# A deformable-attention bias network on one core: every first-layer tile built as a sum and a relu, five of eight by GpSimd and three by VectorE

## The chip, the cores and the metric

The kernel runs on one core of a Trainium2 chip. The metric is the device time of one execution in microseconds. The core has five engines that work side by side and wait for one another on semaphores: TensorE (PE in the profile, its weight loads PEld), VectorE (DVE), ScalarE (ACT), GpSimd (POOL) and SyncE (SP), which here issues the transfers. Operands lie in SBUF (128 partitions); TensorE writes to PSUM (8 banks of 512 fp32 values per partition).

## The reference

The input x is 2 x 256 x 32 x 32. A first layer computes queries, then offsets for an 8 x 8 grid of sampling points per image and group (16 image-group pairs, "groups" below), samples the input there, and makes keys and values. The part that matters here is the position bias: for each of 16 groups, each of 1024 pixels i and each of 64 points j,

```
pos  = grid_q[i] - grid_kv[j]                      # two coordinates
bias = sign(pos) * log1p(|pos|)                    # two coordinates
bias = relu(bias @ cpb_w1 + cpb_b1)                # 2 -> 64 channels
bias = relu(bias @ cpb_w2 + cpb_b2)                # 64 -> 64
bias = bias @ cpb_w3 + cpb_b3                      # 64 -> 1
sim  = q k^T + bias ; softmax over j ; times v
```

Then come an output projection, an MLP with GELU, and a second layer with full self-attention over 1024 tokens, 8 heads of 32, two images. All data is fp32.

## The kernel before, in words

**Stages.** Lines are those of the profile. A head (queries, convolution of the offsets, sampling) fills the first 91 us. The bias network (the loop at L917 on TensorE, L481 on ScalarE, L678 on VectorE, L359 on GpSimd) follows, then the first attention (L935 on), projection and MLP (L986 on), and the second attention.

**First layer of the bias network.** x and y take 32 values per point along their axis, so channel c of pixel (row a, column b) and point j is u(j, b) + v(j, a), with u = w1x * s_x and v = w1y * s_y + b1, where s is the signed logarithm. A tile m (0 to 511, 32 per group) is 128 partitions x 1024 values: two points in the upper and lower 64 partitions, two more along the free axis, and half of the pixel rows (512 pixels). U and V2 (in SBUF, two buffers each for a piece of 16 tiles) hold u and v; ScalarE writes them in `first_sums` (L444). V1 (in PSUM) holds -v, written by ScalarE in `first_bounds` (L454).

**Two kinds of tile.** relu(u + v) = max(u, -v) + v. Even tiles use this: VectorE makes max(u, -v) in one operation (`bound1`, L668: u from SBUF, -v from PSUM), and TensorE adds the missing W2^T v to the second layer's sum with `offset` (L889), four bf16 matmuls with 57 rows, whose operands are the three-part bf16 split of the logarithms (S, 128 x 4096 bf16, filled by GpSimd at L342 and by six transfers at L263) and a matrix wl1 made in the head (L822, L593 to L599, L856, L654). The split itself is L646, L648, L649 and L651 on VectorE. In odd tiles GpSimd writes u + v to SBUF (L370, both inputs in SBUF), and VectorE applies the relu in place, SBUF to SBUF (`relu1`, L674).

**The rest of the loop.** `layer2` (L898) is four fp32 matmuls 64 x 64 x 512 per tile into z2, a ring of 3 x 2 banks; ScalarE's `relu2` (L479) reads it and writes h2, a ring of 8; for four tiles at a time `layer3` (L907) makes 16 fp32 matmuls into bank 7, and after 32 tiles VectorE copies that bank to BT (L692). h1, the ring between first and second layer, has 4 tiles (HRING). 

**What orders the work.** Each engine's program is written out in order of m. VectorE waits in `relu1(m)` for GpSimd's add (z1_added). GpSimd's add of tile m waits for `layer2` of tile m-4 (z2_ready, the ring) and, at L366, for VectorE's h1_ready of m-1, that is until the relu of tile m-2 is done:

```
                if m >= HRING:
                    pool.wait_ge(z2_ready, m - HRING + 1)
                if m >= 2:
                    pool.wait_ge(h1_ready, m - 1)
```

**In the head.** The sampling weights wsm (8 tiles k of 128 x 1024) are hat functions made by ScalarE (L436, L438), then multiplied by hx: k = 0 to 3 by GpSimd (L355), k = 4 to 7 by VectorE (L659), the latter behind the split of the logarithms in VectorE's program. TensorE takes each with 32 small matmuls (L868); after the last one kv_ready is set, on which keys and values (L466 to L474) and the loop depend. SP sends the logarithms to memory (L266) and reads them back broadcast (L256, raw), sends and places the bf16 parts (L260, L263), and then issues the late weights (L286).

Of the kernel before, what the change touches and what calls it, by code (L numbers as in the profile page):

```python
# [44 lines left out]
WS_POOL = 4  # L45
# [12 lines left out]
def build(nc, d, out):  # L58
# [5 lines left out]
    with ctx:  # L64
# [96 lines left out]
        def v(name, i=0, n=1):  # L161
# [4 lines left out]
        ld_vec, ld_bd, ld_w1, ld_late, ld_w2 = (sem(x) for x in ("ld_vec", "ld_bd", "ld_w1", "ld_late", "ld_w2"))  # L166
# [6 lines left out]
        grid_out, grid_in, w1p_ready, wl1_ready, wl1_saved = (sem(x) for x in ("grid_out", "grid_in", "w1p_ready", "wl1_ready", "wl1_saved"))  # L173
        pn_ready, ln_ready, sparts_ready, s_in = (sem(x) for x in ("pn_ready", "ln_ready", "sparts_ready", "s_in"))
        s_out = [sem(f"s_out{a}") for a in range(3)]
        ws_ready, kv_ready, kv_saved, k_ready, v_ready, k_saved, v_saved = (
            sem(x) for x in ("ws_ready", "kv_ready", "kv_saved", "k_ready", "v_ready", "k_saved", "v_saved"))
        abs_ready, hat_ready, ws_pool = sem("abs_ready"), sem("hat_ready"), sem("ws_pool")
        q_copied, qk_ready = sem("q_copied"), sem("qk_ready")
        raw_in, u_ready, v_ready1, z1_added, h1_ready, z2_ready, h2_ready, l3_done = (  # L180
            sem(x) for x in ("raw_in", "u_ready", "v_ready1", "z1_added", "h1_ready", "z2_ready", "h2_ready", "l3_done"))
        sf_ready, sf_out, fold_ready, fold_saved, neg_ready = (
            sem(x) for x in ("sf_ready", "sf_out", "fold_ready", "fold_saved", "neg_ready"))
# [39 lines left out]

        block = ctx.enter_context(nc.Block())
# [108 lines left out]
        def _(pool):  # L333
# [6 lines left out]
            pool.wait_ge(ld_vec, 64)  # L340
            for i in range(2):
                pool.tensor_copy(S[:, 8 * i:8 * (i + 1), :, :].rearrange("p g a b -> p (g a) b"),  # L342
                                 v("one_rows").unsqueeze(2).to_broadcast((P, 8 * CHUNKS, W))).then_inc(cleared, 1)


# [6 lines left out]

            for k in range(WS_POOL):
                pool.wait_ge(hat_ready, k + 2)
                pool.tensor_tensor(wsm[:, k, :], wsm[:, k, :], hx[:, :], ALU.mult).then_inc(ws_pool, 1)  # L355


            pool.wait_ge(kv_ready, 1)
            for m in range(1, PAIRS * G, 2):  # L359
                c, w, hf = m % PAIRS // 4, m % 4 // 2, m % 2  # L360
                if m % PIECE == 1:
                    pool.wait_ge(u_ready, 2 * (m // PIECE + 1))
                if m >= HRING:
# [3 lines left out]
                shape, i = (P, 2, HALF // W, W), m // PIECE % 2  # L367
# [807 lines left out]
```

## Time and profile before

| | |
|---|---|
| median of 3 runs | 1402.49 us (1401.1 to 1406.26) |
| the profiled execution | 1401.21 us, its span 1399.0 us |
| PE busy | 1302.2 us (93% of the span) |
| DVE, ACT, POOL busy | 921.5, 967.6, 748.9 us (66, 69, 54%) |
| mean granted TensorE clock | 0.974 |
| bias loop, from its first matmul (L889) to the last copy (L692) | 90.89 to 841.20 us |

The span runs from the first to the last instruction of the profiled execution; 2.2 us of its time lie around it. PE's busy share is that of the modelled matmul ends. PEclk is the granted TensorE clock in tenths of full speed. "Idle before" names the time in which an engine stood still just before an instruction, and behind the arrow what released it.

### The profile page before, as it was taken

The page shows a single profiled execution, that of the slowest core. Times are in us where ns is not written, and L with a number is a line of the kernel's source. Part 1 is how long each engine was busy: PE and PEld are TensorE (multiplying, and loading weights), DVE is VectorE, ACT ScalarE, POOL GpSimd, SP SyncE. Part 2 cuts the span into 40 slices and gives each one's busy share as a digit, 9 for nine tenths or more (in the row PEclk, how much of TensorE's full clock was granted, in tenths as well). Part 3 has the DMA queues.
Part 4 walks back from the last instruction along what each step waited for, and adds up shares of the span by engine and source line. Part 5 has one row for each costly group of instructions (what it writes and reads, how often), then busy time and mean ns, then how long its engine had stood idle before and what let it go on. Part 6 is the DMA issues. An engine that isn't in the chain of part 4 may idle for free.

```text
span 1399.0 us, 29958 instructions
## 1 busy us (share of the span) xinstructions
PE 1302.2 (93%) x11666; PEld 616.0 (44%) x11666; DVE 921.5 (66%) x1270; ACT 967.6 (69%) x1263; POOL 748.9 (54%) x681
## 2 busy tenths in 40 slices
PE   3169999999999999999999998799997999999998
PEld 2132222222222222222222226444454888888885
DVE  6876666666666666666666657410037999999995
ACT  3377777777777777777777773332204999999994
POOL 4166666666666666666666652200000767777772
PEclk9579999999999999999999999999999999999999
DMA  2141110111011101110111000000007222212211
GB/s 69 54 134 31 31 32 2 31 31 32 2 31 32 29 4 32 31 26 7 31 32 23 9 1 1 1 0 0 0 29 272 62 60 60 54 45 52 60 30 60
DMA packets 19922, 53.27 MB, mean 38 GB/s; under 512 B 4642, under 2 KB 7330, under 8 KB 19668
## 3 DMA queue, kind: packets, MB, share of 16 engines
q1 hardware_dynamic: 19824, 51.92, 14.1%
q8 instruction: 70, 1.15, 0.4%
q14 instruction: 24, 0.20, 0.0%
q10 hardware_dynamic: 4, 0.01, 0.0%
HBM read 40.95 MB, written 10.95 MB: 37 GB/s over the span
## 4 chain that ended last, share of the span: by engine, by line
PE 80%; DVE 11%; issue 3%; ACT 2%; POOL 2%; DMA 1%; SPq 1%; DVEq 0%; ACTq 0%; POOLq 0%
PE ps L898 31%; PE ps L907 17%; PE ps L889 5%; DVE aneg L773 5%; PE ps L1055 4%; PE ps L1063 4%; PE ps L1004 4%; PE ps L1014 4%; PE ps L1047 3%; DVE conv L620 2%; PE ps L1038 1%; DVE big L776 1%; POOL big L355 1%; PE ps L1026 1%; PE ps L991 1%
## 5 line engine op out<-in xcount | busy, mean ns | idle before, releaser
L898 PE MATMUL ps<-big,w 64*64 64x512 f32 x4096 | 483.5, 589 | 0.0
L479 ACT ACTIVATE big<-ps 128x1024 f32<-128x1024 f32 x256 | 262.0, 1023 | 179.0 <-PE ps L898 179.0
L674 DVE TENSOR_SCALAR big<-big 128x1024 f32<-128x1024 f32 x256 | 177.8, 694 | 263.8 <-POOL big L370 263.8
L668 DVE TENSOR_TENSOR big<-qpad,ps 128x1024 f32<-128x1024 f32 x256 | 311.0, 1215 | 7.8 <-ACT ps L458 5.4
L370 POOL TENSOR_TENSOR big<-qpad 128x1024 f32<-128x1024 f32 x128 | 244.5, 1910 | 133.2 <-PE ps L898 68.6
L370 POOL TENSOR_TENSOR big<-qpad,V 128x1024 f32<-128x1024 f32 x128 | 244.5, 1910 | 129.7 <-PE ps L898 73.5
L479 ACT ACTIVATE big<-ps,vec 128x1024 f32<-128x1024 f32 x256 | 284.0, 1109 | 0.0
L390 POOL TENSOR_TENSOR big<-BT,big 128x512 f16<-128x512 f32 x129 | 150.4, 1166 | 248.0 <-DVE big L776 248.0
L907 PE MATMUL ps<-big,w3s 128*32 128x512 f32 x2048 | 246.2, 598 | 1.3 <-ACT big L479 1.3
L898 PEld LDWEIGHTS ps<-big,w 64*64 64x64 f32 x4096 | 146.6, 133 | 205.9 <-issue 112.6
L773 DVE TENSOR_REDUCE aneg<-ps 128x1 f32<-128x1024 f32 x131 | 158.3, 1209 | 6.0 <-PE ps L1047 5.7
L535 ACT ACTIVATE big<-ps,aneg 128x1024 f32<-128x1024 f32 x130 | 148.5, 1142 | 6.0 <-DVE aneg L773 5.3
L1055 PE MATMUL ps<-ident,big 128*128 128x128 f32 x1032 | 136.3, 274 | 3.8 <-DVE big L779 3.8
L907 PEld LDWEIGHTS ps<-big,w3s 128*32 128x32 f32 x2048 | 53.5, 109 | 181.7 <-ACT big L479 92.2
L1055 PEld LDWEIGHTS ps<-ident,big 128*128 128x128 f32 x1032 | 121.1, 141 | 23.2 <-DVE big L779 5.7
L1063 PE MATMUL ps<-BT,big 128*128 x2048 | 115.6, 208 | 1.1
L1063 PEld LDWEIGHTS ps<-BT,big 128*128 128x128 f16 x2048 | 99.0, 97 | 21.3 <-issue 10.3
L889 PE MATMUL ps<-S,wl 57*64 57x512 bf16 x1024 | 102.3, 389 | 1.5 <-ACT vs L474 1.5
L1047 PE MATMUL ps<-h1l,h1h 128*128 128x512 f32 x262 | 94.5, 443 | 6.8 <-DMA h1l<-k_d 5.2
L889 PEld LDWEIGHTS ps<-S,wl 57*64 57x64 bf16 x1024 | 29.5, 105 | 144.7 <-ACT big L479 80.7
L779 DVE SCALAR_TENSOR_TENSOR big<-ps,big 128x512 f16<-128x512 f32 x129 | 89.1, 691 | 0.8 <-ACT big L543 0.4
L540 ACT ACTIVATE BT<-ps 128x512 f32<-128x512 f32 x129 | 79.1, 613 | 4.0 <-PE ps L1055 4.0
(140 smaller groups left out, 1116.5 us busy)
## 6 DMA issues: line engine op xcount, KB each, us to landing
raw<-s_f SPq DMA_DIRECT2D x32, 512.0 KB, 6.1
h1h<-q_d SPq DMA_DIRECT2D x64, 128.0 KB, 3.0
h1l<-k_d SPq DMA_DIRECT2D x64, 128.0 KB, 3.1
q_d<-XN SPq DMA_DIRECT2D x8, 512.0 KB, 2.6
k_d<-XN SPq DMA_DIRECT2D x8, 512.0 KB, 2.6
X<-in_x SPq DMA_DIRECT2D x2, 1024.0 KB, 6.3
out<-X SPq DMA_DIRECT2D x8, 256.0 KB, 2.0
m<-grid_d SPq DMA_DIRECT2D x1, 1024.0 KB, 4.6
```

Of the source, the lines that this page charges most:

```text
L370: pool.tensor_tensor(h1[m % HRING].rearrange("p (y a b) -> p y a b", y=2, b=W), u.unsqueeze(2).to_broadcast(shape), a[:, :, HALF // W * hf ...
L390: pool.tensor_tensor(PTL[u % 2][:, 0:HALF], PF[u % 2], PTH[u % 2][:, 0:HALF], ALU.subtract).then_inc(pFl_ready, 1)
L479: act.activation(h2[m % H2RING], z2[m % ZRING], ACT.Relu, bias=v("cb2") if m % 2 else 0.0).then_inc(h2_ready, 1)
L535: act.activation(PR[u % 2], bank(2 * (u % 2), 2), ACT.Exp, bias=aneg[u % 2][:, :]).then_inc(pr_ready, 1)
L668: dve.tensor_tensor(h1[m % HRING].rearrange("p (y a b) -> p y a b", y=2, b=W), u.unsqueeze(2).to_broadcast(shape), b[:, :, HALF // W * hf: ...
L674: dve.tensor_scalar(h1[m % HRING], h1[m % HRING], 0.0, None, ALU.max).then_inc(h1_ready, 1)
L773: dve.tensor_reduce(aneg[u % 2][:, :], bank(2 * (u % 2), 2), AX.X, ALU.max, negate=True).then_inc(mx_ready, 1)
L889: pe.matmul(z2[m % ZRING][CH * y:CH * (y + 1), HALF * x:HALF * (x + 1)], wl1[CH * x:CH * x + KROWS, 2 * w + y, :], S[CH * x:CH * x + KROWS ...
L898: last = pe.matmul(z2[m % ZRING][CH * y:CH * (y + 1), HALF * x:HALF * (x + 1)], w2[CH * x:CH * (x + 1), :], h1[m % HRING][CH * x:CH * (x + ...
L907: last = pe.matmul(zb[32 * k:32 * (k + 1), :], w3s[:, a:a + 32], h2[(m + k // 2) % H2RING][:, HALF * (k % 2):HALF * (k % 2 + 1)], start=(m ...
L1055: last = pe.transpose(bank(4 + hf)[:, P * i:P * (i + 1)], PR[u % 2][:, P * jt:P * (jt + 1)], ident[:, :])
L1063: last = pe.matmul(bank(6 + u % 2)[:, 0:VW], pT[u % 2][:, P * jt:P * (jt + 1)], V3[:, 2 * k + u // NK, jt, :], start=(jt == order[0] and p ...
```

## The change

It drops the max trick and its bf16 product. Every tile is now u + v followed by `relu1` on VectorE. Of each eight tiles, numbers 1, 4 and 6 have their sum made by VectorE (`add1`: u from SBUF, +v from V1 in PSUM), the other five by GpSimd (both inputs in SBUF). VectorE issues the sum of tile m+1 ahead of the relu of tile m. The ring h1 grows from 4 to 6 tiles (a new buffer h1x). GpSimd no longer waits for VectorE's relu; it waits for the ring and for its own previous sum. `relu2` has the bias in every tile. In the head the fold of w1y through W2, the matrix wl1, the three-part split, its six placing transfers and S are gone, and all eight products of wsm go to VectorE.

```diff
-HRING, H2RING, BURST, ZRING = 4, 8, 4, 3
-PARTS_S = [0, 0, 1, 1, 0, 2]
...
+HRING, H2RING, BURST, ZRING = 6, 8, 4, 3
+OWN = 8
+ON_DVE = (1, 4, 6)
...
-WS_POOL = 4
...
-        h1 = [big[:, 4 + i, :] for i in range(HRING)]
+        h1x = sb("h1x", [P, 2, N])
+        h1 = [big[:, 4 + i, :] for i in range(4)] + [h1x[:, i, :] for i in range(2)]
...
+        def dve_built(m):
+
+            return sum(1 for i in range(m) if i % OWN in ON_DVE)
+
+        def pool_built(m):
+
+            return m - dve_built(m)
...
@@ SyncE
-            send(0)
             sp.wait_ge(sf_out, 16)
             load_raw(0)
-            sp.wait_ge(s_out[0], 16)
-            sp.wait_ge(cleared, 7)
-            rows = [[r for r in range(NR) if PARTS_S[r] == a] for a in range(3)]
-            for a in range(3):
...
-            sp.wait_ge(ws_pool, WS_POOL)
-            sp.wait_ge(ws_ready, NK - WS_POOL)
+            sp.wait_ge(ws_ready, NK)
             sp.wait_ge(q_copied, T)
-            sp.wait_ge(wl1_saved, 1)
@@ GpSimd
-            for k in range(WS_POOL):
-                pool.wait_ge(hat_ready, k + 2)
-                pool.tensor_tensor(wsm[:, k, :], wsm[:, k, :], hx[:, :], ALU.mult).then_inc(ws_pool, 1)
-
-
             pool.wait_ge(kv_ready, 1)
-            for m in range(1, PAIRS * G, 2):
-                c, w, hf = m % PAIRS // 4, m % 4 // 2, m % 2
-                if m % PIECE == 1:
+            for m in range(PAIRS * G):
+                if m % OWN not in ON_DVE:
+                    c, w, hf = m % PAIRS // 4, m % 4 // 2, m % 2
                     pool.wait_ge(u_ready, 2 * (m // PIECE + 1))
-                if m >= HRING:
-                    pool.wait_ge(z2_ready, m - HRING + 1)
-                if m >= 2:
-                    pool.wait_ge(h1_ready, m - 1)
+                    if m >= HRING:
+                        pool.wait_ge(z2_ready, m - HRING + 1)
+                    if m > 0:
+                        pool.wait_ge(z1_pool, pool_built(m))
...
@@ ScalarE
-                    act.wait_ge(h1_ready, PIECE * p - 1)
-                act.activation(V1.rearrange("p (k n) -> p k n", k=4), piece(p, 1), ACT.Identity, scale=neg[:, 0:1],
-                               bias=neg[:, 1:2]).then_inc(v_ready1, 1)
+                    act.wait_ge(z1_dve, dve_built(PIECE * p))
+                act.activation(V1.rearrange("p (k n) -> p k n", k=4), piece(p, 1), ACT.Identity, scale=v("cw1y"),
+                               bias=v("cb1")).then_inc(v_ready1, 1)
...
-                act.activation(h2[m % H2RING], z2[m % ZRING], ACT.Relu, bias=v("cb2") if m % 2 else 0.0).then_inc(h2_ready, 1)
+                act.activation(h2[m % H2RING], z2[m % ZRING], ACT.Relu, bias=v("cb2")).then_inc(h2_ready, 1)
@@ VectorE
-            dve.tensor_copy(spt[0], s3).then_inc(sparts_ready, 1)
...
-            dve.wait_ge(wl1_ready, 1)
-            dve.tensor_copy(wl1[:, :, :], bank(0)[:, 0:4 * CH].rearrange("p (k c) -> p k c", k=4)).then_inc(wl1_saved, 1)
-
             dve.wait_ge(hat_ready, 1)
-            for k in range(WS_POOL, NK):
+            for k in range(NK):
...
-            def bound1(m):
+            def add1(m):
...
+                if m >= HRING:
+                    dve.wait_ge(z2_ready, m - HRING + 1)
...
-                                  b[:, :, HALF // W * hf:HALF // W * (hf + 1)].unsqueeze(3).to_broadcast(shape), ALU.max).then_inc(h1_ready, 1)
+                                  b[:, :, HALF // W * hf:HALF // W * (hf + 1)].unsqueeze(3).to_broadcast(shape), ALU.add).then_inc(z1_dve, 1)
...
-                    if m % 2 == 1:
-                        relu1(m)
-                    else:
-                        if m >= HRING:
-                            dve.wait_ge(z2_ready, m - HRING + 1)
-                        bound1(m)
+                    if m + 1 < PAIRS * G and (m + 1) % OWN in ON_DVE:
+                        add1(m + 1)
+                    relu1(m)
@@ TensorE
-            def offset(m):
...
-                                         start=(m % 2 == 1), stop=True, skip_group_check=True)
+                                         start=True, stop=True, skip_group_check=True)
...
-                    if m % 2 == 0:
-                        offset(m)
                     pe.wait_ge(h1_ready, m + 1)
                     layer2(m)
```

## Rows read from the trace of the kernel before

**Rows 1.** Page: busy time, share of the span and instructions of each engine.

```profile
PE 1302.2 (93%) x11666; PEld 616.0 (44%) x11666; DVE 921.5 (66%) x1270; ACT 967.6 (69%) x1263; POOL 748.9 (54%) x681
```

**Rows 2.** Busy time by stretch: PE, PEld, DVE, ACT, POOL, then granted clock.

```profile
200.00:400.00 200.00, 200.00 (x1920) 58.44 (x1916) 128.35 (x142) 152.61 (x163) 130.53 (x69) 1.00 0.12 28
...
880.00:900.00 20.00, 14.60 (x76) 8.75 (x74) 9.38 (x21) 7.91 (x13) 7.53 (x8) 0.83 0.00 0
```

**Rows 3.** Chain that ended last: shares of the span by line.

```profile
PE ps L898 31%; PE ps L907 17%; PE ps L889 5%; DVE aneg L773 5%; PE ps L1055 4%; PE ps L1063 4%; PE ps L1004 4%; PE ps L1014 4%; PE ps L1047 3%; DVE conv L620 2%; PE ps L1038 1%; DVE big L776 1%; POOL big L355 1%; PE ps L1026 1%; PE ps L991 1%
```

**Rows 4.** Timeline (start, length, instruction, idle before): the loop's start and end.

```profile
79.75 1.06 ACT L438 ACTIVATE big<-big 128x1024 f32<-128x1024 f32 x1
...
82.22 4.50 PE L868 MATMUL ps<-big 128*32 128x64 f32 x160 [2.21 <-POOL big L355]
...
90.89 0.41 PE L889 MATMUL ps<-S,wl 57*64 57x512 bf16 x4 [1.53 <-ACT vs L474]
...
841.20 0.69 DVE L692 COPY BT<-ps 128x512 f32<-128x512 f32 x1 [6.38 <-PE ps L907]
```

**Rows 5.** Timeline inside the loop, VectorE and GpSimd.

```profile
299.90 1.91 POOL L370 TENSOR_TENSOR big<-qpad,V 128x1024 f32<-128x1024 f32 x1 [1.13 <-PE ps L898]
...
301.85 0.69 DVE L674 TENSOR_SCALAR big<-big 128x1024 f32<-128x1024 f32 x1 [1.22 <-POOL big L370]
...
302.45 1.22 DVE L668 TENSOR_TENSOR big<-qpad,ps 128x1024 f32<-128x1024 f32 x1
302.69 1.91 POOL L370 TENSOR_TENSOR big<-qpad,V 128x1024 f32<-128x1024 f32 x1 [0.87 <-DVE big L674]
```

**Rows 6.** Costliest groups: line, engine, operands, count, busy us, mean ns, idle before.

```profile
L674 DVE TENSOR_SCALAR big<-big 128x1024 f32<-128x1024 f32 x256 | 177.8, 694 | 263.8 <-POOL big L370 263.8
L668 DVE TENSOR_TENSOR big<-qpad,ps 128x1024 f32<-128x1024 f32 x256 | 311.0, 1215 | 7.8 <-ACT ps L458 5.4
L370 POOL TENSOR_TENSOR big<-qpad 128x1024 f32<-128x1024 f32 x128 | 244.5, 1910 | 133.2 <-PE ps L898 68.6
...
L479 ACT ACTIVATE big<-ps,vec 128x1024 f32<-128x1024 f32 x256 | 284.0, 1109 | 0.0
```

**Rows 7.** Timeline of the head, DVE: split of the logarithms, products of wsm.

```profile
64.00 1.22 DVE L646 CAST qpad<-BT 32x2048 bf16<-32x2048 f32 x1
65.25 2.28 DVE L648 TENSOR_TENSOR BT<-BT,qpad 32x2048 f32<-32x2048 f32 x1
67.57 3.27 DVE L649 CAST qpad<-BT 32x2048 bf16<-32x2048 f32 x1
70.87 4.32 DVE L651 TENSOR_TENSOR qpad<-BT,qpad 32x2048 bf16<-32x2048 f32 x1
75.12 0.41 DVE L654 CAST wl<-ps 128x256 bf16<-128x256 f32 x1
75.45 1.20 DVE L659 TENSOR_TENSOR big<-big,m 128x1024 f32<-128x1024 f32 x1
76.59 3.37 DVE L659 TENSOR_TENSOR big<-big,m 128x1024 f32<-128x1024 f32 x1
```

**Rows 8.** The same stretch, POOL: its four products of wsm.

```profile
65.99 3.76 POOL L355 TENSOR_TENSOR big<-big,m 128x1024 f32<-128x1024 f32 x1 [36.31 <-ACT big L438]
69.71 3.34 POOL L355 TENSOR_TENSOR big<-big,m 128x1024 f32<-128x1024 f32 x1
73.01 5.87 POOL L355 TENSOR_TENSOR big<-big,m 128x1024 f32<-128x1024 f32 x1
78.83 3.34 POOL L355 TENSOR_TENSOR big<-big,m 128x1024 f32<-128x1024 f32 x1
```

**Rows 9.** ScalarE's preparation of a piece, 150 to 900 us: longest of three kinds.

```profile
L451 ACT ACTIVATE V<-raw,vec 128x512 f32<-128x512 f32 x15 | 12.2, 810 | 0.0
```

**Rows 10.** Waits of GpSimd on itself: us in total, times, longest.

```profile
POOL big L397 <- POOL BT L395: 23.6, 128, 0.2
```

**Rows 11.** The fold in the head: longest of VectorE's seven small operations.

```profile
L595 DVE CAST w1p<-w1s 2x64 bf16<-2x64 f32 x1 | 1.6, 1643 | 0.0
```

More of the change, by code:

```diff
@@ L163, in v @@
             return vec[:, a:a + n]
-        ld_vec, ld_bd, ld_w1, ld_late, ld_w2 = (sem(x) for x in ("ld_vec", "ld_bd", "ld_w1", "ld_late", "ld_w2"))
+        ld_vec, ld_bd, ld_late, ld_w2 = (sem(x) for x in ("ld_vec", "ld_bd", "ld_late", "ld_w2"))
         ld_x = [sem(f"ld_x{b}") for b in range(B)]
@@ L172, in build @@
         pwl_ready, pw_ready, off_ready, gxy_ready = (sem(x) for x in ("pwl_ready", "pw_ready", "off_ready", "gxy_ready"))
[L173 to L175 removed]
+        grid_out, grid_in = sem("grid_out"), sem("grid_in")
+        pn_ready, ln_ready = sem("pn_ready"), sem("ln_ready")
         ws_ready, kv_ready, kv_saved, k_ready, v_ready, k_saved, v_saved = (
             sem(x) for x in ("ws_ready", "kv_ready", "kv_saved", "k_ready", "v_ready", "k_saved", "v_saved"))
[L178 removed]
+        abs_ready, hat_ready = sem("abs_ready"), sem("hat_ready")
         q_copied, qk_ready = sem("q_copied"), sem("qk_ready")
[L180 to L183, printed above, removed]
+        raw_in, u_ready, v_ready1, z1_pool, z1_dve, h1_ready, z2_ready, h2_ready, l3_done = (
+            sem(x) for x in ("raw_in", "u_ready", "v_ready1", "z1_pool", "z1_dve", "h1_ready", "z2_ready", "h2_ready", "l3_done"))
+        sf_ready, sf_out = sem("sf_ready"), sem("sf_out")
         bias_saved, w3_ready = sem("bias_saved"), sem("w3_ready")
@@ L338, in _ @@
                 pool.memset(m, 0.0).then_inc(kv_cleared, 1)
[L340 to L343, printed above, removed]
             pool.wait_ge(q_saved, 2 * T)
@@ L820, in _ @@
             pe.wait_ge(ld_vec, 64)
-            pe.wait_ge(ld_w2, 16 * 3)
-            pe.matmul(bank(7)[0:2, 0:CH], v("cw1y", 0, 2)[0:CH, :], w2[0:CH, :], start=True, stop=False)
-            pe.matmul(bank(7)[0:2, 0:CH], v("zero", 0, 2)[0:CH, :], ident[0:CH, 0:CH], start=False, stop=True).then_inc(fold_ready, 1)
             pe.wait_ge(ld_bd, 16 * 3 * HP)
@@ L848, in _ @@
             last.then_inc(pw_ready, 1)
-            pe.wait_ge(w1p_ready, 1)
-            pe.wait_ge(ld_w1, 16)
-            pe.wait_ge(off_ready, 1)
-            for k in range(4):
-                for h in range(2):
-                    for a in range(3):
-                        last = pe.matmul(bank(0)[CH * h:CH * (h + 1), CH * k:CH * (k + 1)], sel[:, a, k, :], w1f[:, a, :],
-                                         start=(a == 0), stop=(a == 2))
-            last.then_inc(wl1_ready, 1)
             for k in range(NK):
-                if k < WS_POOL:
-                    pe.wait_ge(ws_pool, k + 1)
-                else:
-                    pe.wait_ge(ws_ready, k + 1 - WS_POOL)
+                pe.wait_ge(ws_ready, k + 1)
                 for t in range(T):
@@ L881, in _ @@
             last.then_inc(v_ready, 1)
-            def offset(m):
-                g, c, w, hf = m // PAIRS, m % PAIRS // 4, m % 4 // 2, m % 2
-                rows = HALF // W
-                for y in range(2):
-                    for x in range(2):
-                        pe.matmul(z2[m % ZRING][CH * y:CH * (y + 1), HALF * x:HALF * (x + 1)],
-                                  wl1[CH * x:CH * x + KROWS, 2 * w + y, :],
-                                  S[CH * x:CH * x + KROWS, g, c, rows * hf:rows * (hf + 1)].unsqueeze(2).to_broadcast((KROWS, rows, W)),
-                                  start=True, stop=False, skip_group_check=True)
             def layer2(m):
@@ L1139 @@
         rep(a[L0 + "cpb_w1"].T, 2), rep(a[L0 + "cpb_b1"].reshape(CH, 1), 2), _np.zeros((P, 1), _np.float32),
-        rep(a[L0 + "cpb_b2"].reshape(CH, 1), 2), rep(a[L0 + "cpb_w3"], 2), (part % 16 // 3 == 2).astype(_np.float32).reshape(P, 1),
+        rep(a[L0 + "cpb_b2"].reshape(CH, 1), 2), rep(a[L0 + "cpb_w3"], 2),
         rep(a[L0 + "cpb_b3"].reshape(1, 1), P),
@@ L1144 @@
         (4 * _np.arange(NK)[None, :] + (part // W)[:, None]).astype(_np.float32)], axis=1)
-    sel = _np.zeros((2, 3, 4, CH), _np.float32)
-    for w in range(2):
-        for y in range(2):
-            for r in range(NR):
-                sel[0, PARTS_W[r], 2 * w + y, 32 * w + 16 * y + r] = 1.0
-            for r in range(3):
-                sel[1, r, 2 * w + y, 32 * w + 16 * y + NR + r] = 1.0
     perm = _np.zeros((P, P), _np.float32)
```

75 lines of the change are left out of this document (16 added, 59 removed).

## The prediction

> **What bounds the kernel now.** I read the page first: TensorE is busy 93% of the span at a mean granted clock of 0.974 [rows 1]. The stretches then show where it is full: between 200 and 400 us it is busy 200 of 200 us at clock 1.00, while VectorE, ScalarE and GpSimd have a quarter to a third of their time free [rows 2]. The chain that ended last gives 31% of the span to layer 2, 17% to layer 3 and 5% to the bf16 product of the even tiles [rows 3]. So the bias loop is TensorE's. From 90.89 us to 841.20 us [rows 4] it takes 750 us for 512 tiles, or 1.465 us a tile. By the chain's shares of 1399 us, four tiles take TensorE 0.31 x 1399 / 128 = 3.4 us of layer 2, 1.86 of layer 3 and 0.55 of bf16 product, 5.8 us together, and it does not wait.
>
> The timeline shows a second thing, on which all below rests: GpSimd's sum and VectorE's relu never lie side by side [rows 5]. The sum runs from 299.90 to 301.81, the relu from 301.85 to 302.54, the next sum starts at 302.69. VectorE's relu waits for the sum (263.8 us in all [rows 6]), and the sum waits for the relu before it. What does lie beside the sum is VectorE's max, which reads one operand from PSUM: it starts at 302.45 beside a sum, and in all 256 instances the two means stay at 1215 and 1910 ns [rows 6].
>
> **The two engines in the head.** There they do run side by side, and these rows price the change. VectorE's cast of 32 x 2048 takes 1.22 us at 64.00, with GpSimd idle; the same form at 67.57 takes 3.27 us [rows 7]. GpSimd's first product ends at 69.75 [rows 8], and the cast ends at 70.84, 1.09 us later: it waited for the product's end and then ran whole. GpSimd is held in the same way: its second product starts at 69.71, and ends at 73.05, 2.2 us after the cast; its first ends 2.2 us after the subtraction L648 (67.53), its last 2.2 us after a VectorE product (79.96). So two operands in SBUF on GpSimd and a VectorE operation that uses both of its paths to SBUF exclude one another for an instruction's whole length, in both directions. The cast moves 2048 values in 1.22 us, 1.7 a nanosecond; the relu L674, SBUF to SBUF, moves 1024 in 0.694 us, 1.5 a nanosecond, against 0.84 for the max, which reads PSUM [rows 6]. The relu is thus of the fast kind, as the cast is, and I take it to exclude GpSimd too. The Trainium skill says this as a rule (SBUF — State Buffer, Who interferes with whom): a VectorE instruction in a 2-port mode, tensor_scalar among them, and a GpSimd instruction share one port pair as an exclusive lock, and the second one fully blocks. The head's rows agree. By that rule the loop is bound by the port; without it, it would be the 1327 us of the first rival. One row departs from its "whoever starts first": GpSimd's third product stood from 73.01, VectorE's L651 ended at 75.19, yet a VectorE product begun at 75.45 went ahead of it [rows 7, 8]. Such a turn changes the order, not the sum.
>
> **The change, part by part, for eight tiles of the loop.** Before they take 11.7 us.
> - TensorE loses two offsets per four tiles: 5% of 1399 us, some 70 us in all. It needs 5.29 x 2 = 10.6 us for eight tiles.
> - ScalarE: the bias in all tiles makes a relu2 1.109 us [rows 6]; starts back to back are about 0.09 closer than the lengths, as VectorE's in rows 5 show, so 1.02. With three preparations for a piece of 16 tiles, each of at most 0.81 us [rows 9], that is 8 x 1.02 + 1.2 = 9.4 us. Covered by TensorE, and more so by what follows.
> - VectorE: eight relus and three sums. A relu takes 0.60 from start to next start (301.85 to 302.45 [rows 5]). The new sum is not in the trace; its nearest row is the max of the same operands, 1.22, so 1.13 between starts. Bounds 0.6 (the relu) and 1.3. Total 8 x 0.60 + 3 x 1.13 = 8.2 us: below TensorE.
> - GpSimd: five sums of 1.91, 9.55 us. The new wait on its own previous sum costs 0.18 each (23.6 us over 128 [rows 10]): 10.45 us, just below TensorE. Behind this wait stands only the next sum.
> - What is dropped is L366, the wait for VectorE's relu, which kept the two apart. Now they may meet, and they must take turns: 9.55 + 8 x 0.60 = 14.35 us for eight tiles if every VectorE sum lies beside a GpSimd sum and nothing else is lost. If no VectorE sum finds a GpSimd sum beside it, 17.7 us. Below, the floor loses perhaps 0.8 us if the start of a held instruction is hidden (the held cast saved 0.13 of 1.22): 13.55 us.
> - Between the ends the ring decides. GpSimd may be six tiles ahead, so it draws level with the ring and then waits for layer 2 of tile m-6, which follows the relu by 0.86 us, or by 2.7 behind layer 3. I laid 27 tiles out with these lengths, each sum starting when ring, own wait and port allow. One stretch of eight, from the end of relu 19 at 34.6: relu 20 to 35.2; sum 24 to 37.1 (VectorE's sum 22 inside); relu 21 to 37.7; sum 26 to 39.6; relu 22 to 40.2; sum 27 to 42.1; relu 23 to 42.7; VectorE's sum 25 to 43.8, GpSimd idle until layer 2 of tile 23 at 43.6; sum 29 to 45.5; relus 24, 25, 26 to 47.3; sum 28 on VectorE, GpSimd idle to 47.8; sum 31 to 49.7; relu 27 to 50.3. That is 15.7 us: 14.35 and 1.4 in which the port lies idle. Three such stretches took 46.8 us together, 1.95 us a tile.
> - The loop: 512 x 1.95 = 998 us against 750, **+248 us**. TensorE then waits in each tile, so its 70 us are worth nothing.
> - Head: the split (64.00 to 75.5) leaves VectorE, which is free for all eight products. They follow ScalarE's hats, the last at 80.81 [rows 4]; a product takes 1.20 undisturbed [rows 7], so it ends near 82.0. TensorE has then one step of 32 matmuls left, a fifth of the 4.50 us that five steps took after 82.22 [rows 4]: kv_ready at 83.0 instead of 86.7. **-3.7 us**, between 0 and -4.
> - At nothing: the fold on TensorE and VectorE (under TensorE's wait for the transferred weights), GpSimd's fill of S (GpSimd then waits for TensorE's transposes), ScalarE's small transfer, the six placing transfers and three sends on SP's queue. SP passes to raw and the late weights earlier; the latter are not needed until the MLP. If the cover went, the fold would give back some 3 us: its longest operation takes 1.6 [rows 11], the rest about 0.2 each. The wait of `first_bounds` for VectorE's sum 14 stands ahead of relu2 of tile 13, which comes later anyway.
>
> The sum against the profiled execution: 1401.2 + 248 - 3.7 = 1645.5; the median lies 1.3 us above it. I round to **1645 us**.
>
> **Rivals.**
> - *No exclusion between this relu and this sum.* Then TensorE stays the bound: 1401 - 70 - 4 = 1327 us, faster. GpSimd's chain of 10.45 against 10.6 just holds. For it: the loop's own rows never show relu and sum together, so the relu's case is inferred from the cast. Against: the fast rate, and both directions of holding in the head. It decides where eight relus add over 2.15 us to GpSimd's 9.55, which is when the sum passes the 11.7 of before; that needs only 0.27 us a relu of the 0.60.
> - *Partial exclusion*: GpSimd's broadcast reads leave gaps in which a relu passes, at half to four fifths of its 4.8 us for eight tiles: 12 to 13.4 us, 768 to 858 us for the loop: 1415 to 1505.
> - *TensorE's clock falls too.* It will be busy 10.6 of 15.6 us, 68%. At 880 to 900 us it was busy 14.6 of 20, and the mean clock was 0.83 [rows 2]. At the lower level (1.2 GHz) eight tiles need 21.2 us, 1355 us for the loop: near 2000; at clock 0.83 on average 12.7 us, still under the port, with z2 later and the port idler: 1700 to 1780.
> - *Poor overlap*: 17.7 us, 1133 us for the loop, 1780 us. Within the forecast's own case.
>
> **Chances.** Exclusion as forecast 0.85; clock well down besides 0.04; partial 0.04; none 0.07. The range: the floor of 14.35 gives 918 us and 1565; the lower floor gives 867 and 1514; the top is 1780. I take 1545 to 1760, which holds the forecast's case save its ends. A measurement of this kernel tells 0.5% (7 us) from no change. Faster 0.07, slower 0.92, same 0.01.
>
> **What the profile of the changed kernel would show.** L370's successor well above 1.91 us in the mean (held by relus: towards 2.5 to 3) and relu1 above 0.694 (towards 1.5 to 2), while add1 stays near 1.22; TensorE idle about a third of the loop, released by VectorE's relu; the loop some 1000 us long; the first loop matmul near 87 us; the stretches after it unchanged. I am wrong if relu1 keeps 0.69 and GpSimd 1.91 while they overlap in the timeline; if TensorE's clock is near half in the loop; or if ScalarE releases TensorE.

## The result and the profile after

The changed kernel took 1639.3 us (median of 4 runs, 1636.49 to 1641.04) against 1404.38 us before (4 runs, 1401.1 to 1406.44): a ratio of 1.1673, 95% interval 1.1641 to 1.1706, **235 us slower**. 1645 had been forecast, with a range of 1545 to 1760. The profiled execution has a span of 1638.2 us against 1399.0.

Of the page of the changed kernel, the busy totals, the granted clock, the chain by line, and the groups of the loop:

```profile
PE 1338.2 (82%) x10590; PEld 581.8 (36%) x10590; DVE 1372.2 (84%) x1454; ACT 1009.9 (62%) x1263; POOL 904.9 (55%) x739
...
PEclk8589999999999999999999999999999989999999
...
DVE big L616 17%; DVE h1x L616 8%; DVE big L607 6%; PE ps L804 6%; PE ps L813 5%; DVE aneg L709 4%; PE ps L958 3%; ACT big L435 3%; PE ps L966 3%; PE ps L907 3%; PE ps L917 3%; DVE h1x L607 3%; PE ps L950 2%; DVE conv L566 2%; ACT ps L415 1%
...
L616 DVE TENSOR_SCALAR big<-big 128x1024 f32<-128x1024 f32 x342 | 491.8, 1472 | 0.8 <-POOL big L328 0.8
L804 PE MATMUL ps<-big,w 64*64 64x512 f32 x2736 | 366.1, 623 | 136.4 <-DVE big L616 104.6
L328 POOL TENSOR_TENSOR big<-qpad 128x1024 f32<-128x1024 f32 x107 | 223.3, 2087 | 161.0 <-PE ps L804 99.8
...
L607 DVE TENSOR_TENSOR big<-qpad,ps 128x1024 f32<-128x1024 f32 x128 | 154.7, 1209 | 27.0 <-ACT ps L415 25.8
```

Layer 2 and layer 3 had 48% of the chain before [rows 3]; now they have 11% (L804, L813), and VectorE's relu (L616) and sum (L607) lead. The relu is the same instruction on operands of the same shape as the L674 of rows 6, where it took 694 ns in the mean; here it takes 1472. Yet its idle time fell from 263.8 us to 0.8: what was a wait on a semaphore is now inside the instruction. VectorE's sum, with one operand in PSUM, is at 1209 ns, as the max was at 1215. GpSimd's sum rose only from 1910 to 2087 (2.08 us over all its groups).

Busy time by stretch (PE, PEld, DVE, ACT, POOL, granted clock) for 200 us of the loop, to set beside rows 2:

```profile
200.00:400.00 200.00, 155.94 (x1248) 36.59 (x1248) 200.00 (x147) 124.78 (x124) 132.80 (x65) 0.99 0.07 17
```

TensorE went from 200 to 156 us, VectorE from 128 to 200. How that comes about is seen in the timeline, single instructions of VectorE and GpSimd in order of time (start, length, instruction, idle before):

```profile
298.91 1.26 DVE L616 TENSOR_SCALAR big<-big 128x1024 f32<-128x1024 f32 x1
299.80 2.15 POOL L328 TENSOR_TENSOR big<-qpad,V 128x1024 f32<-128x1024 f32 x1 [0.17 <-POOL h1x L328]
300.10 2.40 DVE L616 TENSOR_SCALAR big<-big 128x1024 f32<-128x1024 f32 x1
302.11 2.15 POOL L328 TENSOR_TENSOR big<-qpad,V 128x1024 f32<-128x1024 f32 x1 [0.17 <-POOL big L328]
302.42 2.40 DVE L616 TENSOR_SCALAR big<-big 128x1024 f32<-128x1024 f32 x1
```

The sum ends at 301.95; the relu begun at 300.10 ends at 302.50, 0.55 us later. The next sum, begun at 302.11, ends at 304.26, the next relu at 304.82, 0.56 later. In this stretch they alternate strictly. One relu occupies VectorE for 2.4 us and works for 0.6. Over the loop the relus range from 678 to 2424 ns; over 40% of them (219 of 512) stay below 0.7 us.

By the three parts of the span: the loop, from its first matmul at 90.17 to its last copy at 1078.55, takes 988.4 us against 750.3, **+238.1**; it starts 0.7 us earlier; what follows takes 559.7 us against 557.8, +1.9. The sum, +239.3, is the span's difference. Tiles come every 1.93 us (1.95 forecast), eight in 15.44.

The head's end, in the timeline of TensorE and VectorE:

```profile
83.63 1.08 PE L785 MATMUL ps<-big 128*32 128x64 f32 x32 [1.05 <-DVE big L594]
84.78 1.22 DVE L607 TENSOR_TENSOR big<-qpad,ps 128x1024 f32<-128x1024 f32 x1 [1.20 <-PE ps L785]
...
87.11 1.98 PE L796 MATMUL ps<-vw,kvs 128*64 128x128 f32 x16
...
90.17 2.84 PE L804 MATMUL ps<-big,w 64*64 64x512 f32 x12 [1.08 <-ACT vs L430]
```

kv_ready came at 84.7 instead of 86.7, but the stretch from there to the loop grew from 4.2 to 5.5 us. The granted clock (third number from the end) says why. Busy time by stretch, the kernel before:

```profile
86.00:88.00 2.00, 1.50 (x35) 1.26 (x28) 1.21 (x1) 0.38 (x1) 1.17 (x1) 0.71 1.02 349
88.00:90.00 2.00, 1.35 (x19) 1.04 (x18) 1.23 (x3) 1.54 (x5) 1.19 (x2) 1.00 1.01 390
```

And the changed kernel:

```profile
88.00:90.00 2.00, 1.09 (x12) 0.69 (x8) 2.00 (x2) 1.51 (x4) 1.86 (x2) 0.50 1.02 375
90.00:92.00 2.00, 1.83 (x12) 0.71 (x16) 2.00 (x1) 0.00 (x0) 1.86 (x2) 0.50 1.10 404
```

Before, TensorE had just run 160 matmuls in a row (4.50 us [rows 4]); now it gets the same matmuls 32 at a time with 1.05 us of waiting between, and stays at 1.2 GHz for the key and value matmuls (1.98 us for the sixteen of L796, 1.09 for the same sixteen before) and for the first layer 2 of the loop. The traces of the runs below agree: with the head of before (e5, e10) the granted clock is at 1.00 by 88 us, as in the kernel before; with the new head, in the ten other runs, the stretch from kv_ready to the loop takes 5.5 us each time.

### The profile page after: what moved, and what is told of

Its sections match the earlier page's. It is cut to its first block, busy times and chain, and to the rows that moved or that the text cites. A ratio compares the mean times of both kernels' runs of the same rounds, so it can differ in the third digit from the quotient of the medians.

```text
span 1638.2 us, 28511 instructions
## 1 busy us (share of the span) xinstructions
PE 1338.2 (82%) x10590; PEld 581.8 (36%) x10590; DVE 1372.2 (84%) x1454; ACT 1009.9 (62%) x1263; POOL 904.9 (55%) x739
## 4 chain that ended last, share of the span: by engine, by line
DVE 43%; PE 33%; issue 14%; ACT 7%; POOL 1%; DMA 0%; SPq 0%; DVEq 0%; ACTq 0%; POOLq 0%
DVE big L616 17%; DVE h1x L616 8%; DVE big L607 6%; PE ps L804 6%; PE ps L813 5%; DVE aneg L709 4%; PE ps L958 3%; ACT big L435 3%; PE ps L966 3%; PE ps L907 3%; PE ps L917 3%; DVE h1x L607 3%; PE ps L950 2%; DVE conv L566 2%; ACT ps L415 1%
## 5 line engine op out<-in xcount | busy, mean ns | idle before, releaser
L435 ACT ACTIVATE big<-ps,vec 128x1024 f32<-128x1024 f32 x512 | 554.2, 1113 | 375.2 <-PE ps L804 373.7
L616 DVE TENSOR_SCALAR big<-big 128x1024 f32<-128x1024 f32 x342 | 491.8, 1472 | 0.8 <-POOL big L328 0.8
L804 PE MATMUL ps<-big,w 64*64 64x512 f32 x2736 | 366.1, 623 | 136.4 <-DVE big L616 104.6
L328 POOL TENSOR_TENSOR big<-qpad 128x1024 f32<-128x1024 f32 x107 | 223.3, 2087 | 161.0 <-PE ps L804 99.8
L813 PE MATMUL ps<-big,w3s 128*32 128x512 f32 x2048 | 258.6, 624 | 1.4 <-ACT big L435 1.4
L616 DVE TENSOR_SCALAR h1x<-h1x 128x1024 f32<-128x1024 f32 x170 | 250.4, 1492 | 0.0
L804 PE MATMUL ps<-h1x,w 64*64 64x512 f32 x1360 | 184.3, 622 | 68.8 <-DVE h1x L616 53.7
L804 PEld LDWEIGHTS ps<-big,w 64*64 64x64 f32 x2736 | 86.8, 133 | 399.6 <-issue 212.8
L607 DVE TENSOR_TENSOR big<-qpad,ps 128x1024 f32<-128x1024 f32 x128 | 154.7, 1209 | 27.0 <-ACT ps L415 25.8
L709 DVE TENSOR_REDUCE aneg<-ps 128x1 f32<-128x1024 f32 x131 | 158.3, 1209 | 5.8 <-PE ps L950 5.6
L328 POOL TENSOR_TENSOR h1x<-qpad,V 128x1024 f32<-128x1024 f32 x53 | 110.1, 2077 | 56.3 <-PE ps L804 52.9
L328 POOL TENSOR_TENSOR h1x<-qpad 128x1024 f32<-128x1024 f32 x53 | 110.2, 2080 | 48.2 <-PE ps L804 44.0
L813 PEld LDWEIGHTS ps<-big,w3s 128*32 128x32 f32 x2048 | 55.2, 113 | 204.7 <-issue 139.9
L804 PEld LDWEIGHTS ps<-h1x,w 64*64 64x64 f32 x1360 | 42.7, 132 | 200.0 <-issue 103.0
L966 PEld LDWEIGHTS ps<-BT,big 128*128 128x128 f16 x2048 | 99.0, 97 | 21.5 <-issue 10.8
```

Of the source, the lines that this page charges most:

```text
L328: pool.tensor_tensor(h1[m % HRING].rearrange("p (y a b) -> p y a b", y=2, b=W), u.unsqueeze(2).to_broadcast(shape), a[:, :, HALF // W * hf ...
L435: act.activation(h2[m % H2RING], z2[m % ZRING], ACT.Relu, bias=v("cb2")).then_inc(h2_ready, 1)
L607: dve.tensor_tensor(h1[m % HRING].rearrange("p (y a b) -> p y a b", y=2, b=W), u.unsqueeze(2).to_broadcast(shape), b[:, :, HALF // W * hf: ...
L616: dve.tensor_scalar(h1[m % HRING], h1[m % HRING], 0.0, None, ALU.max).then_inc(h1_ready, 1)
L709: dve.tensor_reduce(aneg[u % 2][:, :], bank(2 * (u % 2), 2), AX.X, ALU.max, negate=True).then_inc(mx_ready, 1)
L804: last = pe.matmul(z2[m % ZRING][CH * y:CH * (y + 1), HALF * x:HALF * (x + 1)], w2[CH * x:CH * (x + 1), :], h1[m % HRING][CH * x:CH * (x + ...
```

## The experiments

All are edits of the changed kernel, but e5 and e10 of the kernel before. Where no interval is given, the time is that of one execution. "Loop" is measured as above. The kernel before took 1404.8 to 1405.4 us beside them.

| run | sums by VectorE / GpSimd, of eight | total us | loop us | eight tiles us | relu mean ns |
|---|---|---|---|---|---|
| before | (max trick) 0 / 4 | 1404.4 | 750.3 | 11.72 | 694 |
| after | 3 / 5 | 1639.3 | 988.4 | 15.44 | 1479 |
| e1_share4 | 4 / 4 | 1635.0 | 984.0 | 15.38 | 1420 |
| e2_share3 | 5 / 3 | 1558.9 | 905.1 | 14.14 | 1106 |
| e6_share1 | 7 / 1 | 1563.3 | 911.5 | 14.24 | 852 |
| e3_relu1x | 3 / 5, relu on one path | 1461.1 | 811.2 | 12.68 | 1236 |
| e7_share4_phase | 4 / 4, timed | 1524.3 | 873.3 | 13.65 | 690 |
| e4_turns | 3 / 5, waits of before | 1566.4 | 916.1 | 14.31 | 739 |
| e12_ring8 | 3 / 5, ring 8 | 1654.2 | 1002.5 | 15.66 | 1593 |
| e8_thirds | every third by GpSimd, timed | 1433.7 | 781.0 | 12.20 | 686 |
| e9_thirds8 | the same, ring 8, V1 rewritten two tiles earlier | 1380.0 | 727.9 | 11.37 | 683 |
| e5_mix | 2 max trick, 3 / 3 | 1399.8 | 746.4 | 11.66 | 687 |
| e10_mix7 | the same, ring 7, V1 rewritten two tiles earlier | 1383.0 | 728.8 | 11.39 | 686 |

The relu's mean is taken over its groups in the loop (big and h1x, in some runs also m): over the whole loop for the two kernels, e12 from 95 us on, the others from 150 or 200 us on. Taken from 150 us on, that of the changed kernel is 1449 ns.

**e3_relu1x: a slower relu.** The decisive run. The second output of tensor_scalar, a sum per partition that nobody reads, changes only how the instruction runs (racc is a new buffer for it).

```diff
-                dve.tensor_scalar(h1[m % HRING], h1[m % HRING], 0.0, None, ALU.max).then_inc(h1_ready, 1)
+                dve.tensor_scalar(h1[m % HRING], h1[m % HRING], 0.0, 0.0, ALU.max, ALU.add, accum_out=racc[:, m:m + 1]).then_inc(h1_ready, 1)
```

> The relu is written with an accumulated sum per partition as a second output (not used), which should make it run at one value per cycle and over one path: about 1.15 us between starts instead of 0.60 if alone. The data of h1 is the same. Exclusion: a relu that uses one path need not take turns with GpSimd; VectorE's own work is 8 x 1.15 + 3 x 1.13 = 12.6 us for eight tiles, the sums go back to 1.91 us, no relu is longer than about 1.25 us: 806 us for the loop, 1450 to 1480 in all, although each relu alone is twice as long. Rivals A and B (no exclusion): a relu that is 0.55 us longer cannot help; 1640 or more, up to 1900.

1461.1 us, in the expected range: twice as slow a relu makes the kernel 178 us faster. The groups of the loop from 150 to 900 us, then its timeline, both engines in order of time:

```profile
L617 DVE TENSOR_SCALAR_CACHE_REDUCE big<-big 128x1024 f32<-128x1024 f32 x314 | 375.2, 1236 | 0.0
L329 POOL TENSOR_TENSOR big<-qpad,V 128x1024 f32<-128x1024 f32 x100 | 191.2, 1912 | 60.3 <-PE ps L805 50.1 <-POOL big L329 6.8 <-POOL h1x L329 3.4
```

```profile
302.79 1.22 DVE L617 TENSOR_SCALAR_CACHE_REDUCE h1x<-h1x 128x1024 f32<-128x1024 f32 x1
302.86 1.91 POOL L329 TENSOR_TENSOR big<-qpad 128x1024 f32<-128x1024 f32 x1 [1.60 <-PE ps L805]
303.93 1.22 DVE L617 TENSOR_SCALAR_CACHE_REDUCE big<-big 128x1024 f32<-128x1024 f32 x1
```

Two relus lie beside one sum, none of the three is longer than alone. Eight relus and three sums at 1.14 between starts are 12.5 us; 12.68 was measured. So the 1479 ns of the changed kernel are not its work and not a dependency, since order, waits and ring are the same here. They are the exclusion. The Trainium skill (SBUF — State Buffer, Who interferes with whom) exempts the tensor_scalar form that writes out its accumulator from the 2-port modes; this run agrees, 1236 ns against 694, and beside a sum without either being held.

**e1_share4, e2_share3, e6_share1: fewer sums on GpSimd.**

```diff
-ON_DVE = (1, 4, 6)
+ON_DVE = (1, 3, 5, 7)            # e1_share4
+ON_DVE = (1, 2, 4, 5, 7)         # e2_share3
+ON_DVE = (1, 2, 3, 4, 5, 6, 7)   # e6_share1
```

> VectorE makes four of eight sums (tiles 1, 3, 5, 7) instead of three; nothing else differs from the changed kernel. Theory (exclusion): relu and GpSimd's sum take turns, so eight tiles cost 4 x 1.91 + 8 x 0.60 = 12.4 us at the least; the changed kernel took 15.4 where its floor was 14.35, a factor of 1.08, which gives 13.4 us, 857 us for the loop and some 1510 us. Rival A (GpSimd's own chain of sums, waits and ring is the bound, no exclusion): the time goes with the number of its sums, 15.4 x 4/5 = 12.35, 790 us, some 1440. Rival B (VectorE's own work is the bound): one more sum makes it 1.13 us longer for eight tiles, some 1710.

> VectorE makes five of eight sums (tiles 1, 2, 4, 5, 7), GpSimd three. Exclusion: port 3 x 1.91 + 4.8 = 10.5 us, VectorE's own instructions 4.8 + 5 x 1.13 = 10.45 plus what it is held for; three sums of 1.91 partly beside its five: 12 to 13 us, 770 to 830 for the loop, 1420 to 1480 in all. Rival A (GpSimd's chain): TensorE's 10.6 becomes the bound, about 1330. Rival B (VectorE's own work as it stands, relus of 1.47): 8 x 1.4 + 5.65 = 16.8, over 1700.

> VectorE makes seven of eight sums, GpSimd only the first of each eight. Exclusion: VectorE's own 8 x 0.60 + 7 x 1.13 = 12.7 us for eight tiles with 1.91 of GpSimd nearly hidden beside its sums: 12.7 to 13.3 us, 1465 to 1500 in all, so the best share lies at three or two, not at one. Rival A (GpSimd's chain only): TensorE-bound or VectorE-bound at 12.7, 1465. It separates little by itself; it prices VectorE's instructions (0.60 and 1.13 between starts) with GpSimd nearly out of the way: relu1 near 0.69 us in the median.

All three missed, by 125, 79 to 139 and 63 to 98 us: the theory had the right cause and too low a price. e1's timeline (VectorE, then GpSimd) shows what was left out:

```profile
303.84 1.21 DVE L607 TENSOR_TENSOR big<-qpad,ps 128x1024 f32<-128x1024 f32 x1
304.97 2.80 DVE L616 TENSOR_SCALAR big<-big 128x1024 f32<-128x1024 f32 x2
307.69 1.21 DVE L607 TENSOR_TENSOR big<-qpad,ps 128x1024 f32<-128x1024 f32 x1
```

```profile
304.71 1.91 POOL L328 TENSOR_TENSOR h1x<-qpad,V 128x1024 f32<-128x1024 f32 x1 [1.94 <-PE ps L804]
308.56 1.91 POOL L328 TENSOR_TENSOR big<-qpad,V 128x1024 f32<-128x1024 f32 x1 [1.94 <-PE ps L804]
```

Two tiles take 3.85 us, again and again. GpSimd's sum starts when layer 2 frees a slot of the ring ("<-PE ps L804"), and that comes 0.87 us into VectorE's 1.13 us sum. Only 0.26 of the two lie side by side; the next relu is held for the other 1.6. The floor of 12.4 us supposes them fully side by side. In e6 the one sum left in eight still holds VectorE's relus for 1.3 us per eight tiles (8 x (0.85 - 0.68)). None of the rivals' numbers fits either: VectorE's own work would have made e1 slower, GpSimd's chain would have made e2 TensorE-bound at 1330.

**e7_share4_phase: one more wait.**

```diff
                         pool.wait_ge(z1_pool, pool_built(m))
+                    if m > 0:
+                        pool.wait_ge(h1_ready, m)
```

> e1_share4 with one wait more: GpSimd's sum of tile m (m even) also waits until VectorE's relu of tile m-1 is done, so that it starts together with VectorE's sum of tile m+1 and not 0.27 us before its end. In e1_share4 every two tiles took 3.85 us: sum 1.13 on VectorE, 1.6 held by GpSimd's sum, two relus 1.2. Theory (exclusion, and the ring sets a bad phase): 1.91 of GpSimd's sum with VectorE's 1.13 inside it, two relus 1.2, 0.1 to 0.2 of semaphore: 3.2 to 3.3 us for two tiles, 820 to 845 us for the loop, total 1475 to 1500, relus back at 0.69 in the median. Rival (exclusion costs its full sum whatever the phase; or the ring itself is the bound): an added wait cannot help, 1635 or more.

1524.3 us, above its range (1475 to 1500), yet the added wait takes 111 us off e1. The timeline, both engines in order of time:

```profile
301.76 1.22 DVE L609 TENSOR_TENSOR big<-qpad,ps 128x1024 f32<-128x1024 f32 x1
302.02 1.91 POOL L330 TENSOR_TENSOR big<-qpad 128x1024 f32<-128x1024 f32 x1 [1.50 <-DVE big L618]
303.97 1.30 DVE L618 TENSOR_SCALAR big<-big 128x1024 f32<-128x1024 f32 x2 [0.99 <-POOL big L330]
305.18 1.21 DVE L609 TENSOR_TENSOR h1x<-qpad,ps 128x1024 f32<-128x1024 f32 x1
```

VectorE's sum now lies beside GpSimd's but for its first 0.26 us, the relus are 0.69 us, and two tiles take 3.41 us instead of the 3.2 to 3.3 expected. That first step had been put at 0.1 to 0.2. So the phase is a cause of its own beside the port's load.

**e4_turns and e12_ring8: the changed kernel with the old wait, or a longer ring.** e4 adds `if m >= 2: pool.wait_ge(h1_ready, m - 1)` in front of GpSimd's sum; e12 sets HRING = 8 with two tiles in m2, whose weights are then loaded after the loop.

> The changed kernel, share of five of eight as it is, with the wait of before put back: GpSimd's sum of tile m waits until the relu of tile m-2 is done. Theory (exclusion): the port still has 5 x 1.91 + 8 x 0.60 = 14.35 us to carry, so a wait that only orders the turns changes little: 14.6 to 16 us for eight tiles, total 1590 to 1680; the relus that were 2.4 us long become shorter where the wait is on the semaphore instead. Rival (the loss is that both stand ready at the same time and not the port's load): separated, the loop falls towards TensorE's 10.6, total below 1500.

> The changed kernel with a ring of 8 instead of 6 (the two more tiles in m2, whose weights are loaded after the loop); nothing else. It asks how much of its 15.4 us for eight tiles is the ring and how much the port. Theory (exclusion): 5 x 1.91 + 8 x 0.60 = 14.35 us stay whatever the ring; the idle port of about 1 us may go: 14.4 to 15.4 us, 920 to 988 us for the loop, total 1570 to 1640. Rival (the ring's latency is the bound, since e9_thirds8 gained 54 us from it): towards TensorE's 10.6, total below 1500.

e4 took 14.31 us for eight tiles, next to the 14.35 of the port's load, and 1566 us, below its range. Its timeline, both engines in order of time:

```profile
305.79 0.69 DVE L618 TENSOR_SCALAR big<-big 128x1024 f32<-128x1024 f32 x1 [0.67 <-POOL big L330]
306.39 0.69 DVE L618 TENSOR_SCALAR h1x<-h1x 128x1024 f32<-128x1024 f32 x1
306.65 2.20 POOL L330 TENSOR_TENSOR h1x<-qpad,V 128x1024 f32<-128x1024 f32 x1 [0.90 <-DVE big L618]
307.00 1.21 DVE L609 TENSOR_TENSOR big<-qpad,ps 128x1024 f32<-128x1024 f32 x1
```

The sum begins inside a relu and is held for the rest of it (2.20 us, 1.8 of them after the relu's end at 307.08); the relus wait on the semaphore and are 0.69. By the starts and ends in the trace a relu or a GpSimd sum is under way in 14.1 of the 14.3 us: almost nothing of the port is idle. The loss of the change over before is then 14.31 - 11.72 = 2.6 us for eight tiles from the load and 1.1 from the missing order. It is not cured by order alone. e12 took 15.66 us and 1654: a deeper ring gives nothing (the range was passed by 14 us), so the ring's latency is not the bound of the changed kernel; its relus were held longer instead (1593 ns in the mean).

**e8_thirds, e9_thirds8: a version without collisions.** GpSimd makes every third sum while VectorE makes the two others; then come three relus.

```diff
-OWN = 8
-ON_DVE = (1, 4, 6)
+OWN = 3
+ON_DVE = (1, 2)
...
+                    if m > 0:
+                        pool.wait_ge(h1_ready, m)
...
-                    if m + 1 < PAIRS * G and (m + 1) % OWN in ON_DVE:
-                        add1(m + 1)
+                    if m % OWN == 0:
+                        for i in (m + 1, m + 2):
+                            if i < PAIRS * G:
+                                add1(i)
                     relu1(m)
```

> GpSimd makes the sum of every third tile only and waits until all relus before it are done; VectorE meanwhile makes the next two sums (2 x 1.13 = 2.26 us, longer than GpSimd's 1.91), then three relus. Theory: no relu is ever held, VectorE needs 2.26 + 1.8 = 4.06 us for three tiles, TensorE 3.97: 1.36 us a tile, 695 us for the loop against 750 before, total 1345 to 1375 (V1's rewriting may cost a microsecond or two in some pieces): faster than both kernels. Relu1 0.69 us and GpSimd's sum 1.91 us throughout. If semaphore gaps or V1's rewriting weigh more, up to 1400. Rival (the exclusion is not what costs, but that VectorE makes too much): VectorE has more own work here than in the changed kernel (10.8 against 8.2 us for eight tiles), so it stays above 1560 as e2_share3.

> e8_thirds with a ring of 8 instead of 6 (the two more tiles lie in m2, whose weights are loaded after the loop), and V1 rewritten after relu2 of tile 10 of a piece instead of 12. In e8_thirds the loop took 781 us, 12.2 for eight tiles, VectorE was busy 90% and TensorE 92%, and GpSimd waited for the ring. Theory: no relu was held there, what was lost is the ring's latency; with two tiles more VectorE and TensorE run at 10.8 (VectorE's 4.06 us for three tiles): 10.8 to 11.3 us for eight tiles, 690 to 725 us for the loop, total 1340 to 1375, below both kernels. Rival: the loss in e8_thirds is in V1's rewriting or in ScalarE's relu2, which the ring doesn't reach: 1420 to 1435 as before.

e8: 1433.7 us (1431.0 to 1433.9, 4 executions), ratio to before 1.0193 (1.0176 to 1.021). Better than after by 206 us, but above its range: relus 686 ns and sums 1912, as expected, and yet TensorE busy only 92%. e9, with a ring of 8 tiles and V1 rewritten two tiles earlier, took **1380.0 us** (1378.4 to 1381.9, 4 executions), ratio to before **0.9821 (0.9804 to 0.9837)**, ahead of both kernels. Which part of the 54 us is the ring's and which V1's was not separated by a run. The traces point to the ring: between 150 and 700 us GpSimd waited for it (<-PE ps) 167 us in e8 and 62 in e9, VectorE for V1 only 9 us in e8 and not at all in e9. The loop of e9 by stretch:

```profile
200.00:400.00 200.00, 195.15 (x1704) 53.92 (x1700) 195.52 (x242) 163.68 (x168) 89.97 (x47) 1.00 0.12 28
```

TensorE and VectorE are both at 98%. It missed its range (1340 to 1375) by 5 us: 11.37 us for eight tiles where VectorE's 4.06 for three give 10.8.

**e5_mix, e10_mix7: the kernel before with half of its max tiles replaced.** Kinds of tile in eight: P (GpSimd's sum), D (VectorE's sum, u minus V1, which holds -v) and B (the max with its bf16 product).

```diff
+KINDS = "PDBPDBPD"
+CYCLES = ((0, 1, 2), (3, 4, 5), (6, 7))
...
+                    for i in cycle:
+                        if KINDS[i] != "P":
+                            bound1(e + i)
+                    for i in cycle:
+                        if KINDS[i] != "B":
+                            relu1(e + i)
```

> The kernel before with three kinds of tile in each eight: two with the max trick and the bf16 product (instead of four), three with GpSimd's sum, three with VectorE's sum (u minus V1, which holds -v), the last six with a relu; the ring has 5 tiles; GpSimd's sum waits until the relus before it are done. The head stays as before. TensorE: 10.6 + 2 x 0.28 = 11.1 us for eight tiles against 11.7; VectorE 5 x 1.13 + 6 x 0.60 = 9.3 plus about 1 where one of its sums is shorter than GpSimd's. Theory: TensorE-bound, 713 us for the loop, total 1365 to 1385. If the ring of 5 or V1 holds VectorE back: 1385 to 1410.

> e5_mix with a ring of 7 instead of 5 (two tiles in m2) and V1's rewriting at tile 10. e5_mix took 11.7 us for eight tiles where TensorE's matmuls need 11.1. Theory: the ring's latency made up the difference; with 7 tiles TensorE is the bound at 11.1 to 11.3: 710 to 725 us for the loop, total 1360 to 1380. Rival: TensorE's matmuls really take 11.6 in this mixture: 1395 to 1400 as e5_mix.

e5 came to 1399.8, in its second range (1385 to 1410). e10 took 1383.0 us (1382.0 to 1386.4, 4 executions), ratio 0.985 (0.9833 to 0.9867), 3 us above its range. TensorE is busy 199.5 of 200 us there, at 11.39 us for eight tiles instead of 11.1.

**e11_fold: a guess about the head.** In the profile after, the query matmuls took 9.98 us against 8.60.

```diff
+            pe.wait_ge(ld_w2, 16 * 3)
+            pe.matmul(bank(7)[0:2, 0:CH], v("cw1y", 0, 2)[0:CH, :], w2[0:CH, :], start=True, stop=False)
+            pe.matmul(bank(7)[0:2, 0:CH], v("zero", 0, 2)[0:CH, :], ident[0:CH, 0:CH], start=False, stop=True)
             pe.wait_ge(ld_bd, 16 * 3 * HP)
```

> The changed kernel with the two small fold matmuls of before put back at TensorE's start (64 columns each, into bank 7, nobody reads them). In the changed kernel the 16 query matmuls behind them took 9.98 us and began 1.71 us apart in pairs; before, with the fold in front, 8.60 us and 0.86 soon after the start. Theory: the fold's work 2 us earlier put TensorE at its upper clock level sooner; here 8.6 to 8.8 us again, total 1 to 2 us shorter, which one run can't tell, but the first loop matmul comes 1.2 to 1.6 us earlier than 90.17. Rival: the difference lies in the weights' arrival or the data: 9.98 us again.

They took 9.81 us with the fold back in front, the first loop matmul came at 90.18 as in after, and the total was 1640.0. The guess falls. Over all the profiles the 16 matmuls take from 8.6 to 10.2 us, with the fold 8.6, 9.8, 9.9 and 9.6, without it 8.9 to 10.2: it differs from run to run and the fold does not set it. Somewhere in these sixteen the spacing of the matmuls halves, sooner where they are short in all; what sets that point stays open.

## Why the prediction was right

- **Who is bound.** "Relu and GpSimd's sum exclude one another for an instruction's whole length": right, and the step on which all hung. It had been inferred from a cast in the head (1.22 us alone, 3.27 beside GpSimd [rows 7]); the relu did the same, 0.68 alone and up to 2.42. e3 shows it by taking only the second path away.
- **The price.** 15.7 us in the one stretch written out, 15.6 in the mean of the three, against 15.44 measured; the loop 998 against 988.4. The floor of 14.35 was right as the port's load where waits set the turns (e4: 14.31). In the changed kernel the starts and ends in the trace give 13.6 us for eight tiles with a relu or a GpSimd sum under way and 1.8 with neither. So the load was 0.7 below the 14.35 (the lower floor, 13.55, had allowed for a held instruction's start being hidden) and the idle port some 0.4 above the 1.4 laid out: that 15.7 came so near is in part these two cancelling. The part above the floor was laid to a port idle while GpSimd waits for the ring. e1 and e7 show that this waiting is a phase: the ring's release puts GpSimd's sum late beside VectorE's. Where I later put only a factor (1.08, e1) or an allowance (e2, e6) on the sums of lengths instead of laying the tiles out, the estimates failed by 63 to 139 us.
- **Who waits.** I expected sums "towards 2.5 to 3" us: wrong, they took 2.08. GpSimd is held at most for the rest of a relu, VectorE for the rest of a sum, which is three times as long. The relu's 1.5 to 2 was just missed at its lower end (1.48). add1 at 1.21 was right.
- **TensorE's 70 us** were worth nothing in the changed kernel, as said: busy 156 of 200 us, so idle 22% where about a third was forecast. The clock did not fall much: 0.94 to 1.00 in the loop's stretches from 100 us on, at 77 to 82% busy. The rival in which it does was too dark.
- **V1** was put at nothing. VectorE did stand waiting for its rewriting, 3.2 us at a time, thirteen times between 488 and 858 us, 42 us together (<-ACT ps L415). It cost no time that shows: eight tiles took 15.35 us in that part of the loop, 15.40 before it and 15.60 after it.
- **The head.** -3.7 forecast, -0.7 measured. kv_ready came 2.0 us earlier; the missing 1.7 are mostly the query matmuls' 1.4. Then the clock took another 1.3, which the sum had left out: it priced the 32 last matmuls and not what the burst of 160 had done for those after it. The first loop matmul "near 87 us" came at 90.17.
- **The rivals.** No exclusion (1327) and partial exclusion (1415 to 1505) did not come. Poor overlap, 17.7 us, did not come in the changed kernel.

## What to carry to other kernels

Before work is moved to GpSimd, look for a place in the trace where it already runs beside VectorE, and see whether the instructions there are longer than elsewhere: a wait on a semaphore between the two may be what keeps them from a dearer one. The load of the pair is then the sum of GpSimd's instructions and of VectorE's fast SBUF-to-SBUF ones, and VectorE's work on PSUM operands goes beside GpSimd's for nothing, if a semaphore starts both together (1.21 and 1.91 us side by side in e7). Where two engines exclude one another, a slower form of the short instruction, or one wait more, can be the faster kernel: 178 and 111 us here.

## What the runs showed of the hardware that was not expected

- The accumulating form of the relu (1236 ns, against 694) makes room for GpSimd at no cost to it: its sum went from 2.08 back to 1.91 us. It costs a second small instruction of 0.09 to 0.11 us, which the spacing of 1.14 us between starts already holds.
- A held instruction shows no idle time. VectorE was "busy" 200 of 200 us in a stretch in which over a third of that was waiting inside relus: over the loop 512 x (1.48 - 0.68) = 410 of 988 us.
- In the head a burst of 160 small matmuls had lifted the granted clock from 0.50 to 1.00 by 88 us; the same matmuls, 32 at a time with 1.05 us between, left it at 0.50 until 92.
